# Attention and mixture-of-experts kernel: P V as plain fp32 matmuls in two column tiles, with the row sums of P added up on VectorE and GpSimd

## The reference

```python
xn, ln = layernorm(ctx), layernorm(norm(x))
q = rmsnorm(heads(ln @ Wq.T)) * SCALE            # 4 heads of 64
k, v = heads(concat([xn @ Wkv.T, ln @ Wlkv.T]))  # k goes through rmsnorm
attn = softmax(where(full_mask, q @ k.T, -max))
x = x + (attn @ v) @ Wo.T + bo
...
y = silu(gate) * up @ w2                         # per expert, top 2 of 8
x = x + (y_sel * weights).sum()
```

## Time and profile before

| | before |
|---|---|
| median of 3 runs | 1198.44 us (1197.42 to 1199.52) |
| profiled execution, first to last instruction | 1197.7 us |
| mean granted TensorE clock | 0.946 |
| TensorE matmul, busy | 1054.0 us (88%) |
| VectorE, busy | 774.5 us (65%) |
| ScalarE, busy | 656.9 us (55%) |
| GpSimd, busy | 518.0 us (43%) |

### The profile page before, as it was taken

The page is one execution under the profiler, slowest core; times in us unless marked ns, Lnnn a source line. Parts: engine busy times, 40 slices in busy tenths (PEclk is TensorE's granted clock), DMA queues, the critical chain, the costliest instruction groups (busy, mean ns, idle before and its releaser), DMA issues.

```text
span 1197.7 us, 19749 instructions
## 1 busy us (share of the span) xinstructions
PE 1054.0 (88%) x4904; PEld 761.3 (64%) x4905; DVE 774.5 (65%) x1474; ACT 656.9 (55%) x867; POOL 518.0 (43%) x525
## 2 busy tenths in 40 slices
PE   3688689999999999999999999999866268999994
PEld 2455457667666666766666766666555257888884
DVE  4999777766766866766766676686554813444442
ACT  1455446777777777777677677777522012333321
POOL 4012125454544654644645554465410014555553
PEclk9899879999999999999999999999977569999998
DMA  5222402112131111231211211111266777333332
GB/s 162 62 71 71 172 16 69 53 40 70 53 113 58 60 46 53 66 114 45 71 48 48 70 53 49 57 58 47 67 184 209 265 248 199 52 49 52 53 53 26
DMA packets 84392, 100.41 MB, mean 84 GB/s; under 512 B 11035, under 2 KB 78044, under 8 KB 83836
## 3 DMA queue, kind: packets, MB, share of 16 engines
q1 hardware_dynamic: 73694, 89.20, 22.8%
q0 software_dynamic: 7488, 10.23, 5.3%
q10 hardware_dynamic: 3166, 0.46, 0.3%
HBM read 57.60 MB, written 42.26 MB: 83 GB/s over the span
## 4 chain that ended last, share of the span: by engine, by line
PE 70%; DVE 10%; ACT 7%; DMA 5%; issue 5%; SPq 1%; ACTq 1%; DVEq 0%; POOL 0%; POOLq 0%
PE bM L1177 9%; PE bPV L1241 8%; PE bPV L1239 8%; PE bPV L1249 8%; PE bS L1221 7%; PE bS L1222 7%; ACT PT L642 4%; DVE mpart L867 3%; DMA xin<-x 3%; PE bA L1129 2%; PE bG L1340 2%; PE bH L1357 1%; ACT Ph L648 1%; PE bY L1340 1%; PE bY L1342 1%
## 5 line engine op out<-in xcount | busy, mean ns | idle before, releaser
L482 POOL TENSOR_TENSOR Pl<-PT,Ph 128x1024 fp32r<-128x1024 f32 x96 | 230.8, 2404 | 348.5 <-ACT Ph L648 348.5
L867 DVE TENSOR_REDUCE mpart<-bM 128x1 f32<-128x464 f32 x524 | 310.9, 635 | 87.2 <-PE bM L1177 85.9
L642 ACT ACTIVATE PT<-bS 128x1024 f32<-128x1024 f32 (+1 forms) x240 | 239.4, 998 | 139.3 <-PE bS L1222 139.3
L648 ACT CAST Ph<-PT 128x1024 fp32r<-128x1024 f32 (+1 forms) x240 | 245.5, 1023 | 7.0
L894 DVE TENSOR_TENSOR Pl<-PT,Ph 128x1024 fp32r<-128x1024 f32 x144 | 176.1, 1223 | 104.6 <-ACT Ph L648 104.4
L1221 PE MATMUL bS<-Q,S 128*128 128x512 f32 x464 | 185.9, 401 | 1.4 <-ACT Q L633 0.7
L1239 PE MATMUL bPV<-Ph,V 128*65 128x512 f32 x464 | 184.5, 398 | 0.0
L1222 PE MATMUL bS<-Q,S 128*128 128x512 f32 x464 | 184.0, 396 | 0.0
L1241 PE MATMUL bPV<-Ph,V 128*64 128x512 f32 x464 | 183.1, 395 | 0.0
L1177 PE MATMUL bM<-S,Q 128*128 128x464 f32 (+1 forms) x524 | 165.5, 390 | 10.9 <-DVE mpart L867 8.7
L1249 PE MATMUL bPV<-Pl,V 128*65 128x512 f32 x464 | 146.9, 395 | 0.8
(11 more groups left out here) (210 smaller groups left out, 1537.4 us busy)
## 6 DMA issues: line engine op xcount, KB each, us to landing
W<-wsp_d SPq DMA_DIRECT2D x32, 768.0 KB, 5.8
wraw<-w SPq DMA_DIRECT2D x96, 128.0 KB, 2.2
wsp_d<-whi SPq DMA_DIRECT2D x96, 128.0 KB, 1.7
wsp_d<-wraw SPq DMA_DIRECT2D x96, 128.0 KB, 1.7
v_d<-Vs SPq DMA_DIRECT2D x29, 258.0 KB, 3.3
V<-v_d SPq DMA_DIRECT2D x4, 1870.5 KB, 7.6
xall<-x SPq DMA_DIRECT2D x1, 2048.0 KB, 13.6
xin<-x SPq DMA_DIRECT2D x16, 128.0 KB, 3.8
```

The costliest lines, as they stand in the source:

```text
L482: pool.tensor_tensor(Pl[:, p % 3, :, :], PT[:, p % 3, :, :], Ph[:, p % 3, :, :].bitcast(F32), ALU.subtract)\
L642: act.activation(PT[:, p % 3, 0:w, :], bS[sl][:, 0:w, :], ACT.Exp).then_inc(sem("exp"), 1)
L648: act.copy(Ph[:, p % 3, 0:w, :], PT[:, p % 3, 0:w, :]).then_inc(sem("p_hi"), 1)
L867: dve.tensor_reduce(mpart[:, i, g:g + 1], banks[k % len(banks)][:, 0:PIECE], AX, ALU.max)\
```

## The change

V stays on chip as plain fp32, (partition, head, tile x 64), written by ScalarE straight from PSUM; `v_d`, its 29 stores and 4 loads, the low part of V and the ones column are gone. `Ph` and `Pl` are gone too: `PT`, now with 4 buffers and not 3, is the moving operand itself, plain fp32. Of a pair, the first tile goes to the partitions 0 to 63 of `bPV` and the second to 64 to 127, two column tiles of the array. `outputs` of two pairs stand together, so four such matmuls follow each other; each plain fp32 matmul is carried out as two records, as those of the projections are. The sum of P is made by additions: 7 on GpSimd in `acc_p`, 6 on VectorE in `acc_d`, merged by `z_merge` into `zs`. `o_T` is no transposition now but two plain fp32 matmuls per query tile: with `twin` (two identity blocks below each other, which adds the two column tiles) and with a column of ones for `zs`.

A buffer of `PT` is free for a new exponential when its pair's `outputs` and its addition are both done (`pt_free`).

```diff
-        Ph = sb("Ph", [P, 3, 2, QB * P], F32R, at=pro)
+        acc_d = sb("acc_d", [P, 2, QB * P], at=pro)
+        acc_p = sb("acc_p", [P, 2, QB * P], at=pro)
+        zs = sb("zs", [P, QB * P], at=pro)
...
+        V = sb("V", [P, H, NK * D], at=top)
...
# ScalarE, prologue
-                    act.copy(Vs[:, t.par, :, 0:D], heads(bV[t.par][:, 0, 0:DIM])).then_inc(sem("v_hi"), 1)
+                    act.copy(V[:, :, bass.ds(t.v * D, D)], heads(bV[t.par][:, 0, 0:DIM])).then_inc(sem("v_cp"), 1)
...
# ScalarE, unit
+            def pt_free(u, p):
+                old = p - NPT if p >= NPT else max(q for q in range(NP) if q % NPT == p)
+                since = 1 if p >= NPT else 0
+                act.wait_ge(sem("pv"), NP * (u + since) + old + 1)
+                for name, sums in (("z_p", POOL_SUMS), ("z_d", DVE_SUMS)):
+                    for n, pair in enumerate(sums):
+                        if old in pair:
+                            act.wait_ge(sem(name), len(sums) * (u + since) + n + 1)
...
-                    act.wait_ge(sem("pv"), g + 1)
-                    act.activation(PT[:, p % 3, 0:w, :], bS[sl][:, 0:w, :], ACT.Exp).then_inc(sem("exp"), 1)
+                    pt_free(u, p)
+                    act.activation(PT[:, p % NPT, 0:w, :], bS[sl][:, 0:w, :], ACT.Exp).then_inc(sem("exp"), 1)
...
-                    act.copy(Ph[:, p % 3, 0:w, :], PT[:, p % 3, 0:w, :]).then_inc(sem("p_hi"), 1)
...
# VectorE, prologue
-                    dve.tensor_tensor(Vs[:, t.par, :, D + 1:VW], heads(bV[t.par][:, 0, 0:DIM]),
-                                      Vs[:, t.par, :, 0:D].bitcast(F32), ALU.subtract).then_inc(sem("v_lo"), 1)
...
# VectorE, start of the attention
+                dve.tensor_copy(twin[q * D:(q + 1) * D, :], ident[q * D:(q + 1) * D, q * D:(q + 1) * D])\
...
+            dve.memset(acc_d[:], 1.0).then_inc(sem("z_d"), len(DVE_SUMS))
+            dve.memset(acc_p[:], 1.0).then_inc(sem("z_p"), len(POOL_SUMS))
...
# VectorE, unit (GpSimd has the like with acc_p, POOL_SUMS and no w)
+                one = acc_d[:, 0:w, :] if p < 0 else PT[:, p % NPT, 0:w, :]
+                dve.tensor_tensor(acc_d[:, 0:w, :], one, PT[:, q % NPT, 0:w, :], ALU.add).then_inc(sem("z_d"), 1)
...
+            def z_merge(v):
...
+                dve.tensor_tensor(acc_d[:], acc_d[:], acc_p[:], ALU.add).then_inc(sem("zm"), 1)
+                dve.wait_ge(sem("zm"), v + 1)
+                dve.tensor_tensor(zs[:], acc_d[:, 0, :], acc_d[:, 1, :], ALU.add).then_inc(sem("zs"), 1)
...
                 q_stage(u + 1, (u + 1) % UNITS if last else u + 1)
+                z_merge(u)
+                q_lo(u + 1, (j + 1) % 2)
+                done = 0
+                for k, (before, between, after) in enumerate(PIECES):
+                    n = sum(sum(x) for x in PIECES[:k])
+                    for m in range(before + between + after):
+                        piece(u + 1, n + m, M_BANKS)
...
+                    if k == OUT_AT:
                         o_out(u)
+                    while done < ND and max(DVE_SUMS[done]) < 2 * k:
+                        z_sum(u, done)
+                        done += 1
...
# TensorE
-                    last = pe.transpose(bT[:, 0, i * (D + 1):(i + 1) * (D + 1)], oT_a[0:D + 1, i * P:(i + 1) * P],
-                                        ident[0:D + 1, 0:D + 1])
+                    at = i * (D + 1)
+                    pe.matmul(bT[:, 0, at:at + D], oT_a[:, i * P:(i + 1) * P], twin[:], start=True, stop=True)
+                    last = pe.matmul(bT[:, 0, at + D:at + D + 1], zs[:, i * P:(i + 1) * P], onec[:],
+                                     start=True, stop=True)
...
+                    pe.wait_ge(sem("exp"), NP * u + p + 3)
+                    for b, c in enumerate(range(2 * p, min(2 * p + 2, NK))):
+                        last = pe.matmul(bPV[b * D:(b + 1) * D, 0, :], V[:, h, c * D:(c + 1) * D],
+                                         PT[:, p % NPT, b, :], start=c < 2, stop=c >= NK - 2, skip_group_check=True)
...
+                for k in range(len(PIECES)):
+                    scores(2 * k)
+                    pieces(k, 0)
+                    if 2 * k + 1 < NP:
+                        scores(2 * k + 1)
+                    pieces(k, 1)
+                    if k == 0:
                         q_T(u + 1)
+                    if k == OUT_AT:
                         o_T(u)
+                    if k:
+                        outputs(2 * k - 2)
+                        if 2 * k + 1 >= NP:
+                            c_T(u + 1)
+                        outputs(2 * k - 1)
+                    pieces(k, 2)
                 outputs(NP - 1)
...
-SLOTS = [(p, c) for p in range(3, NP - 1) for c in ((0, 2) if p % 2 else (1,))][:NM // 2]
-POOL_PAIRS = (2, 4, 6, 8, 10, 12)
-DVE_PAIRS = tuple(p for p in range(NP) if p not in POOL_PAIRS)
+PIECES = ((0, 0, 0), (2, 2, 1), (2, 2, 1), (2, 2, 2), (2, 2, 2), (2, 2, 2), (2, 2, 0), (0, 0, 0))
+OUT_AT = 2
+POOL_SUMS = ((0, 1), (-1, 3), (-1, 5), (-1, 6), (-1, 8), (-1, 9), (-1, 11))
+DVE_SUMS = ((2, 4), (-1, 7), (-1, 10), (-1, 12), (-1, 13), (-1, 14))
```

More of the change, by code:

```diff
@@ L37 @@
 NB = NT // QB
-VW = 2 * D + 1
 NP = (NK + 1) // 2
+NPT = 4
 NG = -(-KEYS // 512)
@@ L479, in _ @@
                         u = NB * h + 2 * i + j
[L480 to L485, removed]
+                        for n in range(NZ):
+                            z_sum(u, n)
+                            for ch in range(SHARE * n // NZ, SHARE * (n + 1) // NZ):
                                 split(E // H * h + i, SHARE * j + ch)
@@ L868, in piece @@
                     .then_inc(sem("m_red"), 1)
-            def pieces(v, at):
-                for n in (2 * SLOTS.index(at), 2 * SLOTS.index(at) + 1) if at in SLOTS else ():
-                    piece(v, n, M_BANKS)
             def maxima(v):
@@ L897, in unit @@
             def unit(u, j, last):
                 q_stage(u + 1, (u + 1) % UNITS if last else u + 1)
-                for p in range(NP):
-                    pieces(u + 1, (p, 0))
-                    if p:
-                        p_lo(u, p - 1)
-                    if p == 2:
-                        q_lo(u + 1, (j + 1) % 2)
-                    if p == 4:
-                        o_out(u)
-                    pieces(u + 1, (p, 1))
-                    pieces(u + 1, (p, 2))
-                    if p == SLOTS[-1][0]:
-                        maxima(u + 1)
@@ L912, in unit @@
-                p_lo(u, NP - 1)
+                z_merge(u)
[5 more added lines that the diff above has]
+                        piece(u + 1, n + m, M_BANKS)
+                    if n < NM <= n + before + between + after:
+                        maxima(u + 1)
+                    if k == OUT_AT:
+                        o_out(u)
+                    while done < ND and max(DVE_SUMS[done]) < 2 * k:
+                        z_sum(u, done)
+                        done += 1
@@ L914, in _ @@
+                while done < ND:
+                    z_sum(u, done)
+                    done += 1
             dve.wait_ge(sem("q1w"), 1)
@@ L923, in _ @@
                         unit(NB * h + 2 * i + j, j, h == H - 1 and j == 1)
+            z_merge(UNITS)
             o_out(UNITS)
@@ new lines, in pieces @@
+                def pieces(k, part):
+                    n = sum(sum(x) for x in PIECES[:k]) + sum(PIECES[k][:part])
+                    for m in range(PIECES[k][part]):
+                        piece(u + 1, hn, (j + 1) % 2, n + m, M_BANKS)
+                for k in range(len(PIECES)):
[5 more added lines that the diff above has]
+                    if k == 0:
@@ L1257, in unit @@
                         q_T(u + 1)
-                    pieces((p, 0))
-                    if p == 4:
+                    if k == OUT_AT:
                         o_T(u)
-                    if p >= 2:
-                        outputs(p - 2)
-                    pieces((p, 2))
-                c_T(u + 1)
-                outputs(NP - 2)
+                    if k:
[3 more added lines that the diff above has]
+                        outputs(2 * k - 1)
```

114 lines of the change are left out of this document (40 added, 74 removed).

## The result

| | before | after |
|---|---|---|
| median of 4 runs each | 1197.93 us (1196.78 to 1199.52) | 1307.18 us (1302.62 to 1312.34) |
| span of the profiled execution | 1197.7 us | 1300.9 us |
| mean granted TensorE clock | 0.946 | 0.905 |
| TensorE matmul, busy | 1054.0 us (88%) | 1076.5 us (83%) |
| VectorE, busy | 774.5 us | 752.2 us |

The kernel is slower: after / before is 1.0909, 95% interval 1.0876 to 1.0941. Forecast were 1265 us with a range of 1189 to 1307; the median stands 0.2 us above the upper end. The profile is of the fastest of the four executions, 1302.62 us.

What follows compares the result with a forecast made beforehand. The prediction took TensorE to bound the attention and VectorE the prologue. From 1197.7 us, +48 for longer units, +27 clock, -10 prologue and +2 end gave 1264.7, forecast as 1265 us, range 1189 to 1307.

Steps and rivals of the forecast that it cites:

- TensorE's work: TensorE's instructions in one attention unit, waits left out: 38.3 us after the change, 3.1 less than before.
- n matmuls take n + 1 slots: Outputs in two column tiles overlap but keep issue order: 37 slots of 0.43, 15.9 us a unit.
- the rival with 0.13: Outputs: the two column tiles start together, a group of four takes 4 slots, 3.0 us a unit less; chance 0.13.
- 1190 and 1217: Kernel times in us if both column tiles start together: 1190 with the clock held, 1217 with the clock's 27.
- The drain rival: Each of 16 changes a unit between full array and column tiles drains TensorE, up to 0.16 us: 41, 1306 us; chance 0.12.
- The waits: TensorE's waits in a unit: 8.0 us where there were 2.2, with 3.6 before the scores of pair 8.
- the walk: Stepping the four engines' programs through one attention unit in written order: 43.6 us before the change, 46.4 after.
- The clock: TensorE's clock falls behind the 3.6 us wait in each unit, 3.4 us at half speed losing 1.7: 16 x 1.7 = +27.
- a bound (54 us in all): Upper bound of the clock's loss, 16 x 3.4, if it fell at the start of the unit too.
- After 2.11 us idle it held: Reading of the earlier trace: TensorE's clock held after 2.11 us idle, but fell after 2.60.
- Prologue: VectorE, taken as full there, loses 29 subtractions, -12.3, and gains clearings and small copies, +2.3: -10 us.
- The end, +2: Kernel's end: the last merge is ready 1.2 us later than `oT_a` and `o_T` takes 1.2 more, +2 us.

Runs made afterwards that it cites:

- e3_one: Changed kernel with both key tiles of a pair on partitions 0 to 63 of `bPV`, so no second column tile; 1509.07 us, ratio 1.2569.
- e5_single: e4_midlate with the outputs of each pair by themselves, groups of two matmuls in place of groups of four; 1198.37 us, ratio 0.9983.
- e8_out3: e4_midlate with `o_T` one step later and the clearings moved behind the first `q_stage`; 1151.8 us, ratio 0.96.
- e7_notile: e4_midlate with both key tiles of a pair on partitions 0 to 63 of `bPV`, so no second column tile; 1380.09 us, ratio 1.1494.
- e2_fill: Changed kernel with 14 matmuls whose result nobody reads put into TensorE's long wait before the scores of pair 8; 1262.36 us, ratio 1.0516.
- e6_prodve: e4_midlate with one extra VectorE instruction in each of the 29 prologue steps, where the old subtraction stood; 1188.56 us, ratio 0.99.
- e4_midlate: e1_mid with the first pieces one step later and the addition of pair 10 also ahead of the reductions; 1183.43 us, ratio 0.987.
- e1_mid: Changed kernel with two of VectorE's additions per unit placed ahead of a step's last reductions, not behind them; 1218.6 us, ratio 1.0148.

## Why the prediction came out as it did

**TensorE's work, 38.3 us a unit for 41.4: near in its sum, by two errors that cancel.** "n matmuls take n + 1 slots" is wrong. The weight loads at 423.86, 424.35 and 424.77 come two at a time, 0.49 and 0.42 apart, so two tiles start together and four matmuls take 4 slots; this was the rival with 0.13, and e3_one and e5_single bear it out. But its 1190 and 1217 left out what a group costs at its edges: 0.09 ahead, 0.15 at its end, 0.11 on the first matmul behind. So a group of four is 4 x 0.43 + 0.35 = 2.07 us, and 2.15 had been forecast: that the two agree is luck. By the traces the work fell by 1.9 in the changed kernel and by 2.5 in e8_out3, where hardly anything waits (0.2), and not by 3.1.

**The drain rival, 16 x 0.16 a unit, has the right size (8 groups x 0.35 = 2.8 us); its cause is open.** In e7_notile and e3_one, with one tile only, the same additions stand (0.33 between scores and group, 0.13 at its end, 0.32 for the piece behind), so they do not belong to the second column tile. But there too the stationary operand is 64 columns wide in the groups and 128 beside them, so a price for that change is not ruled out. The changed kernel's own trace speaks against plain fp32 alone as the cause. In its prologue four records of 256 columns with a 128-wide operand are followed by transposes 0.87 us later, 4 x 0.216 and nothing over. Behind a group of two, transposes begin 1.01 us after its start, 0.15 over the 0.86:

```profile
119.15 1.03 PE L1141 MATMUL bV<-wl,xT 128*128 128x256 f32 x4
120.02 0.60 PE L1152 MATMUL bK<-ident,knat 128*66 128x128 f32 x4
...
404.32 1.08 PE L1244 MATMUL bPV<-PT,V 128*64 128x512 f32 x4
405.33 0.60 PE L1196 MATMUL bT<-ident,cmax 128*1 128x128 f32 x4
```

The Trainium skill (TensorEngine Tiling (Array Packing), Key Properties) says that a change of tiling mode drains the engine. These rows agree with it, but no run here changes the width and nothing else.

**The waits: right.** 3.26 us before the scores of pair 8 (3.6), 0.49 and 1.11 at the start of the unit (0.7 and 1.6), one of 1.58 where 0.7 was expected; by the trace +5.4 a unit (8.0 - 2.2 = 5.8). Without the 2.8 of the clock a unit would be 46.9 us, and the walk gave 46.4.

**The clock: the step that failed.** "The likelier is that it falls in each unit" took one fall of 1.7 us. It costs 3.0 us a unit: 6.8 us at half speed and not 3.4 in 13 of 15 units, as one long fall or as two, and none in the other two. The text had the second fall only as a bound (54 us in all) and only at the start of the unit; half of the second falls stand elsewhere, behind a wait of 1.6 us that the forecast had at 0.7. e2_fill prices all but 0.3 of it at 2.5 in the pitch. "After 2.11 us idle it held" was one row of several: in the same trace it falls where a wait of 2.05 us ends, so the length of a wait alone does not say whether it falls.

```profile
902.19 0.68 PE L1293 MATMUL bFX<-ident,x 128*128 128x128 f32 x2 [2.05 <-DVE x L955]
902.00:904.00 2.00, 1.81 (x6) 1.55 (x7) 1.39 (x6) 0.94 (x3) 0.00 (x0) 0.55 0.34 84
```

In all, +4.7 a unit had been forecast (3.0, of which 0.2 comes of setting the walk's 46.4 against the measured 43.4, and 1.7) and 6.3 came: 16 x 1.6 = 26 of the 36 us by which the span exceeds the forecast, most of it the clock's.

**Prologue: wrong in size.** "While it is the full engine: -12.3" took a busy share of 94% for the bound. With the subtraction gone VectorE's idle time rose from 1.2 to 1.9 us in 20, so it now waits for others in its turn and a step is not shorter by the whole 0.42; e6_prodve prices the subtractions at 5.4. With the clearings, which e8_out3 prices at 2.35 as forecast, -3 was to be had and -2.4 came, where -10 was forecast: 8 us.

**The end, +2,** was +4.4; over all kernels with the change it is 1.8 to 6.0, so it can't be read closer. `o_T` is 1.8 and not 1.44 a unit: its four records for a query tile take 0.44 us where 0.36 was taken from the earlier trace rows. The addition (1.21 to 1.29 for 1.22) and GpSimd's (2.39 for 2.40) are as priced.

**Luck.** That the time came out beside the upper end of the range, 1307, does not bear the range out. That end was the clock's 27 and drains of 41 on top of groups already priced at n + 1 slots; the time came from more clock and less gain in the prologue.

## What to carry to other kernels

Take the order of the engine that is waited for as seriously as its load: VectorE was busy for 58%, and the place of two additions in its program cost 5.1 us a unit, more than the matmuls saved. Where a wait of some us appears once in a period, count the clock twice: by its own fall, and by falls behind shorter waits, eight in 15 units here, of which two or three were left without the long wait. And an engine that is 94% busy gives back its work only as far as the next chain allows; here that was 5.4 of 12.3 us.

## What the hardware showed

- Plain fp32 matmuls of 512 columns in two column tiles start together: 4 of them (8 records) in 1.87 us, in one tile 3.57.
- A group of plain fp32 matmuls with 64 columns of weights, among fp32r ones with 128, costs about 0.35 us besides its records, with one column tile as with two.
- The clock fell with no idle time in the trace, behind 16 small records of `o_T` in 2.69 us (e7_notile: 0.50 from 398 to 400); behind the same 16 in 1.77 us it held (e4_midlate, 1.00).
- The same wait does not always do the same. Behind 3.25 to 3.26 us the clock fell in 13 of 15 units of the changed kernel and held in two; in e3_one it held in four of 15. Waits of 1.0 to 1.3 us lowered it in 2 of 15 units of e1_mid; in the changed kernel waits of 1.1 to 1.65 us lowered it in 8. The Trainium skill (TensorE: Matmul & The Clock Gate, Part 1) names idle gaps between matmuls as what lowers the clock, and says more generally that it goes by how busy the engine has been of late; e7_notile shows a fall without a gap.
